# An edge stage in which VectorE takes the remainder of the edge attributes behind message and one-hot instead of ahead of them

## The reference, cut to what matters

```
ei   = concatenate([x[src], edge_attr])            # 256 + 64 features for each edge
core = maximum(ei @ W1 + b1, 0) @ W2 + b2
gate = sigmoid(ei @ Wg + bg)
agg  = segment_sum(gate * core, dst)               # message, added up by destination
out  = layernorm(agg + x) * gamma + beta
x    = layernorm(x + out)
```

## Time and profile before

| what | us |
|---|---|
| median of the timed runs | 2568.09 |
| lowest and highest of three runs | 2565.17 and 2568.68 |
| span of the profiled execution | 2722.1 |
| TensorE busy in it | 2389.6 (88%) |
| VectorE busy | 2076.2 (76%) |
| ScalarE busy | 1493.1 (55%) |
| GpSimd busy | 1663.0 (61%) |

### The profile page before, as it was taken

How to read it: one execution, slowest core, us unless ns; L and a number is a source line. 1 busy time by engine, 2 the same in 40 slices (tenths; PEclk the granted TensorE clock), 3 DMA queues, 4 the chain that set the end, 5 groups by cost and what they waited for, 6 DMA issues and landing times.

```text
span 2722.1 us, 50965 instructions
## 1 busy us (share of the span) xinstructions
PE 2389.6 (88%) x16049; PEld 1845.0 (68%) x16049; DVE 2076.2 (76%) x4860; ACT 1493.1 (55%) x2727; POOL 1663.0 (61%) x1581
## 2 busy tenths in 40 slices
PE   7879999999999999999899894689888899888864
PEld 3479999999999998888889881245444444444443
DVE  6658888888889888888889998897777763436455
ACT  1157777777767776676767674454665640112123
POOL 0367777777677776667667661456555645666663
PEclk9989999999999999999999996899999999998976
DMA  6555555555555555555555542254455425665542
GB/s 210 207 154 158 161 167 160 161 163 164 157 160 164 165 157 161 164 170 169 164 163 165 161 143 83 80 138 126 119 142 140 126 92 189 209 228 162 188 129 88
DMA packets 276289, 422.45 MB, mean 155 GB/s; under 512 B 127634, under 2 KB 198692, under 8 KB 274004
## 3 DMA queue, kind: packets, MB, share of 16 engines
q0 software_dynamic: 90368, 281.11, 34.6%
q1 hardware_dynamic: 170028, 116.99, 14.3%
q10 hardware_dynamic: 15656, 21.30, 2.3%
HBM read 354.91 MB, written 64.37 MB: 154 GB/s over the span
## 4 chain that ended last, share of the span: by engine, by line
PE 53%; DVE 18%; issue 9%; ACT 8%; another core or an unknown queue 7%; DMA 2%; DVEq 1%; POOL 1%; ACTq 1%; SPq 0%; POOLq 0%
PE banks L972 15%; PE banks L1060 5%; PE banks L949 5%; PE banks L1034 4%; PE banks L1086 3%; PE banks L856 3%; ACT counts L1432 2%; PE banks L1102 2%; PE banks L946 2%; DVE hidden_lo L1767 2%; PE banks L947 2%; ACT hidden_hi L1296 2%; DVE room L1786 2%; PE banks L960 2%
## 5 line engine op out<-in xcount | busy, mean ns | idle before, releaser
L797 POOL DMA_INDIRECT gathered<-p_table,src_t x784 | 807.2, 1030 | 439.7 <-DVE gate L1778 252.8
L797 POOL DMA_INDIRECT gathered<-hop_table,src_t x576 | 585.5, 1017 | 463.1 <-PE banks L1102 174.8
L972 PE MATMUL banks<-w_hi,hidden_hi 128*128 128x256 f32 x1568 | 462.1, 295 | 55.1 <-DVE hidden_lo L1767 48.6
L972 PE MATMUL banks<-w_lo,hidden_hi 128*128 128x256 f32 x1568 | 443.6, 283 | 0.0
L972 PE MATMUL banks<-w_hi,hidden_lo 128*128 128x256 f32 x1568 | 443.5, 283 | 0.0
L1432 ACT CAST counts<-banks 128x686 f32 (+3 forms) x382 | 295.4, 773 | 213.8 <-PE banks L1037 103.8
L1303 ACT CAST msg_hi<-room 128x512 fp32r<-128x512 f32 x392 | 241.8, 617 | 246.4 <-DVE room L1786 209.5
L1767 DVE SCALAR_TENSOR_TENSOR hidden_lo<-banks,hidden_hi 128x512 fp32r<-128x512 f32 x392 | 270.1, 690 | 121.8 <-ACT hidden_hi L1296 68.4
L972 PEld LDWEIGHTS banks<-w_hi,hidden_hi 128*128 128x128 f32 x1568 | 299.6, 191 | 79.0 <-DVE hidden_lo L1767 66.5
L1034 PE MATMUL banks<-codes,low_hot 128*128 128x343 f16 (+3 forms) x958 | 242.2, 337 | 111.2 <-DVE codes L2002 54.6
L1317 ACT ACTIVATE gate<-gate 128x512 f32<-128x512 f32 x392 | 242.3, 632 | 123.0 <-DVE gate L1778 107.1
(11 more groups left out here) (225 smaller groups left out, 5280.3 us busy)
## 6 DMA issues: line engine op xcount, KB each, us to landing
ea<-in_edge_attr SPq DMA_DIRECT2D x196, 128.0 KB
counts_saved<-counts SPq DMA_DIRECT2D x16, 1568.0 KB
ring<-counts_saved SPq DMA_DIRECT2D x16, 1568.0 KB
gathered<-p_table,src_t POOLq DMA_INDIRECT x784
p_table<-p_t ACTq DMA_DIRECT2D x48, 256.0 KB, 4.1
hop_table<-parts SPq DMA_DIRECT2D x12, 896.0 KB
gathered<-hop_table,src_t POOLq DMA_INDIRECT x576
x_saved<-x_room SPq DMA_DIRECT2D x7, 896.0 KB
```

The costliest lines, as they stand in the source:

```text
L797: pool.indirect_dma_start(out=rows[:, n % slots, j, :], out_offset=None, in_=table[:, :], in_offset=bass.IndirectOffsetOnAxis(ap=src_t[:, ...
L972: last = nc.tensor.matmul(banks[:, 4 + half, j % 2 * H:(j % 2 + 1) * H], lhs, rhs, start=False, stop=n == len(products) - 1, skip_group_ch ...
```

## The change

Two lines of VectorE's order move: the remainder of the edge attributes of group g + 4, with a slot of node work, goes from ahead of message to behind one_hot. It is the same instruction with the same waits. The other engines' queues stay as they are.

```diff
@@ step_in_order @@
                 at_group(add_window, i, s, -2)
                 at_group(lower_msg, i, s, -1)
                 node_work_at(0)
-                at_group(lower_ea, i, s, 4)
-                node_work_at(1)
                 at_group(message, i, s, 0)
                 at_group(one_hot, i, s, 0)
+                node_work_at(1)
+                at_group(lower_ea, i, s, 4)
                 node_work_at(2)
                 at_group(lower_hidden(0), i, s, 1)
                 at_group(lower_hidden(1), i, s, 1)
```

## The result

The changed kernel takes 2577.02 us (median of 5 runs, 2571.74 to 2584.25) against 2565.58 for the kernel before on the same chip (5 runs, 2564.61 to 2568.68). The ratio is 1.0041, 95% interval 1.0027 to 1.0054: **slower by about 0.4%, some 11 us**. A later comparison on another chip gave 1.0033 (1.0021 to 1.0044). The forecast was 2546 us, faster; the time lies outside the range.

What follows compares the result with a forecast made beforehand. TensorE was taken as the bound, waiting in the edge stage for VectorE's late hidden_lo. −18.1 (third stretch) and −3.5 (second) made −21.6, so 2568.1 − 22 = 2546 us, range 2534 to 2566.

Steps and rivals of the forecast that it cites:

- lower_ea beside GpSimd's lower_msg: Late groups of the edge stage: a few more meetings, each 0.31 us on GpSimd, off the path; cost 0.
- meetings with GpSimd block wholly: Rival, edge stage: lower_ea or hidden_lo waits out 1.20 us in ten assumed meetings, +12 against −22, so 2558 us; chance 0.06.
- −18.1 in the third stretch: Last 78 groups profiled in the edge stage: TensorE's waits for hidden_lo, 37.3 us less 19.2 that stay, go: 18.1 us.
- the 0.24 us that I added to each: TensorE's recorded waits for hidden_lo: 0.24 us added to each because ends of matmuls are modelled.
- the waits for the first hidden product: TensorE, third stretch: 13.0 us in 11 waits, from gathers and node chunks; gain worth 0 to 13, taken as 0.
- −3.5 in the second stretch: The 39 groups with the first node work: TensorE loses 6.9 us there; half of it, 3.5 us, was to go.
- The 0.25 us a group of TensorE's late signals: First stretch's TensorE waits for hidden_lo, 18.2 us; the same rate was taken to stay in the third stretch.
- the 19.2 us taken off: Third stretch: 78 groups at 0.25 us of TensorE's waits, assumed to stay and subtracted from 37.3 us.
- Recording costs some 154 us: Whole kernel: profiled span 2722.1 us against timed median 2568.09; differences in the profile were carried over unchanged.
- The first stretch "0": First 74 groups of the edge stage, without node work on VectorE: nothing to win, stays at 7.34 us a group.
- Side effects: Load of edge attributes issued about 2 us later, cost 0 to 2 us; its transpose and TensorE's first-hidden-product waits, 0.
- no change: Rival, third stretch: VectorE is the bound whatever the order, removed waits reappear ahead of hidden_lo; 2568 us, chance 0.15.

Runs made afterwards that it cites:

- before, again: The kernel before, unchanged, profiled once more: 2572.61 us on a chip of the result's kind (about 2566 us), 2690.09 us on the second kind (about 2695 us).
- one fill: GpSimd's lower_msg replaced by one constant fill, without and with the change, against the kernel before: 0.9929 and 0.9865 (first kind of chip), 0.9948 and 1.0008 (second).
- second comparison: The changed kernel run once more against the kernel before, first kind of chip: 1.0033, 2575.04 us.
- the pairs with fills: GpSimd's lower_msg replaced by constant fills, each without and with the change, second kind of chip: one fill 0.9948 and 1.0008, two fills 0.9933 and 0.9987.
- lower_ea alone: Only lower_ea moved behind one_hot, node slot left ahead of message, against the kernel before: 1.0088 on the second kind of chip, 0.9996 on the first.
- the slot alone: Only the node slot moved behind one_hot, lower_ea left ahead of message, against the kernel before: 1.0003 and 1.0002 (second kind of chip), 0.9996 (first).

## Why the prediction was wrong

**The step that failed is "lower_ea beside GpSimd's lower_msg", costed at 0.** I read one meeting, of the two instructions in which GpSimd paid 0.31 us and VectorE nothing, and concluded that such a meeting costs 0.31 us off the path. The row itself did not say so. one_hot had 0.46 us left when lower_msg started (1064.67 less 1064.21), so there was no more than that to wait for, and the 0.31 us fits blocking as well as a small delay. It was a meeting in which GpSimd was the one to wait, and I took it for all. The runs put a held instruction at 0.76 us of VectorE's time on average in the kernel before, 1.06 and 1.11 in the changed one and 1.24 with lower_ea between the halves of hidden_lo. The trace of before held the answer: by the same count it has 36 held node pieces with 26.9 us of excess. Their medians are normal, and I had looked only at the instruction that I was going to move past, never at a line's most against its median. The rule of the Trainium skill that I set against the trace (SBUF — State Buffer, "Who interferes with whom") was right: a VectorE instruction with two SBUF inputs and a GpSimd instruction that reads SBUF shut each other out for a whole instruction. The traces agree. Two SBUF inputs are held (lines 1760, 1799, 1903, 1861), hidden_lo with one input from PSUM is not, in any of its 205 meetings in before, again, and no instruction with two SBUF inputs is held by a fill. What I had not looked for is that tensor_scalar with one SBUF input is held as well: line 1858 took up to 1.77 us in the same trace against a median of 0.17, and line 1883 is held even by a fill.

**The rival "meetings with GpSimd block wholly" had the mechanism and the wrong size and place.** I allowed ten meetings, on lower_ea or hidden_lo, at 1.20 us. Only 4 fall on lower_ea. Most of the price is in the node pieces: besides lower_ea 43 instructions are held instead of 36, nearly all of them node pieces, and each for longer (1.02 and 1.08 us instead of 0.76), which makes 16.5 to 19.2 us of the 22 to 25 more. That VectorE's shift brings them to another moment of lower_msg is inferred from the counts. That GpSimd's lower_msg is what takes the gain away is shown by the pair with one fill. On the first kind of chip the second and third stretches are 24.3 us longer with the read than without, at 27.2 us held; with the change (second comparison, 278.2 + 604.4 us) 48.7 us longer, at 52.4 held. By the medians of the whole kernel it is less, some 19 and 43 to 46 us, and with lower_ea between the halves of hidden_lo 70 for 109. So 0.6 to 0.9 of the held time is time.

**The gain was right in mechanism, and in size partly by luck.** −18.1 in the third stretch was forecast; without the read it is −22.6. lower_ea's waits went, and TensorE's fell. But its waits for hidden_lo give 10.1 us of that, or 13.0 with the 0.24 us that I added to each; the waits for the first hidden product, which I had at 0 to 13 and took as 0, give 5.8. With the read, 22 to 25 us more of held time give all of it back, and the two profiles show the third stretch 1 and 5 us longer than before. −3.5 in the second stretch is hardly there: 280.3 to 279.9 and 278.2 us with the read, 274.7 to 276.0 without (first kind).

**What I took from the first stretch was not a property of the kernel.** The 0.25 us a group of TensorE's late signals, which I subtracted from the third stretch, belongs to the second kind of chip: on the first TensorE has no wait for hidden_lo at all in that stretch. Two faults cancelled in part, the 0.24 us added to each wait and the 19.2 us taken off.

**"Recording costs some 154 us" was wrong.** Profiled executions are as long as timed ones on the same chip, to within some 5 us, and the kernel before takes 2694 us and more on some chips. That the first profile came from such a chip fits its groups of 7.34 us, but its chip is not on record. A span 6% above the timed median should have made me ask which program or chip the trace shows before carrying any difference over unchanged.

**The first stretch "0"** held on the first kind (519.0 to 519.7 us). On the second the same move costs 13 to 18 us there, by the pairs with fills and by lower_ea alone; the change as it stands was not timed on it. **Side effects** held: ScalarE waits for the load of the edge attributes 2.2 us in 2 cases, against 1.9 in 2.

**The rival "no change"** had VectorE as the bound in the third stretch. Its busy time there is 542.7 us, 7.05 a group, in before, again, just above TensorE's 7.01, and 558.1 and 561.4 in the two profiles of the change, where it holds the instructions that are kept waiting. With one fill and the change it is 516.8, and the change gains. So VectorE's own work is not the bound there; with the held time it is as long as TensorE's.

**What stays open in the net result.** The traces show why the gain is absent; the loss beyond that is bounded less well. In the second comparison the medians are 7.7 us apart, but the two profiled executions, 2571.91 and 2572.61 us, are not: that of before lies 5.3 us above its median and that of the change 3.1 below. Held against it, the third stretch of the change is 1 and 5 us longer. The trace of the slot alone is a better measure, since that kernel is as fast as before and its profiled execution is its median: its third stretch is 594.3 us. Against this the change is 6 and 10 us longer there and within 1.1 us in the first two stretches. That puts most of the 8 to 11 us into the third stretch, but across chips and by single profiles, so it isn't shown.

## What to carry to other kernels

When an instruction with two SBUF inputs is moved on VectorE, look up where GpSimd's SBUF-reading instructions run, and ask what else on VectorE will arrive there once the queue has shifted; here a meeting with a GpSimd instruction of 1.20 us cost VectorE 0.8 to 1.2 us on average and up to 1.7, and not the 0.31 us of the one example. Compare the longest with the median of every line before pricing contention by one example: a median hides 36 hits of 0.8 us. And where a producer on another engine can be moved earlier instead of the consumer later, try that first; here it gave the only gain.

## What the runs showed of the hardware

- A VectorE instruction with two SBUF inputs that meets a GpSimd instruction of 1.20 us with SBUF inputs ends just behind its end: 0.03 to 0.04 us for line 1861 with at most 14 elements a partition, 0.29 for lower_ea with 256, 0.56 for line 1792 with 512 (second comparison). It does so even where VectorE's recorded start is up to 0.6 us earlier. lower_ea took up to 2.08 us in the changed kernel and 2.13 with lower_ea between the halves of hidden_lo, for 0.42 of work. Tiny ones are hit alike: line 1861 took up to 1.81 us against a median of 0.17. In before, again none of the 205 hidden_lo, 283 add_gate and 29 batch-norm instructions that ran beside a lower_msg was held by as much as 0.1 us.
- A GpSimd fill of 0.54 us held tensor_scalar instructions with one SBUF input: line 1883 took 0.53 us against 0.16 with one fill and the change.
- The same program takes 2566 or 2695 us depending on the chip, with the granted clock at its upper level (2.4 GHz) in nearly all of the edge stage in both; what sets them apart was not found. The longer one spends 0.3 us more in each group of the first stretch, and 1073 to 1091 us instead of 978 to 983 behind the 195th one_hot. The sign of a change of half a per cent can differ between them: lower_ea alone gave 0.9996 and 1.0088.
